# First attention of a decoder layer: loop body rotated by half a tile on all engines, output projection in the values' bank, residual sum and normalisation behind the query remainder

## The chip, the cores and the metric

The kernel runs on one core of a Trainium2 chip. Its time is the device time of one execution in microseconds, from the profiler's clock; the lower the better. Each engine works through its own queue in order: TensorE (PE, matrix products and transposes, results in the PSUM banks), VectorE (DVE), ScalarE (ACT), GpSimd (POOL) and SyncE (SP, which only issues transfers here). They wait for each other by counting semaphores.

## What is computed

A decoder layer on x (16 sequences of 64 tokens, 512 wide, float32): two attentions and a clustered dense layer, each followed by a residual sum and a normalisation. The change lies in the first attention alone.

```python
def attn(x, Wq, Wk, Wv, Wo):            # 32 query heads, 8 key/value heads, 16 wide
    xq = rope((x @ Wq).reshape(b, s, 32, 16))
    xk = rope((x @ Wk).reshape(b, s, 8, 16))
    xv = (x @ Wv).reshape(b, s, 8, 16)
    xk, xv = repeat(xk, 4), repeat(xv, 4)
    scores = where(causal, einsum('bqhd,bkhd->bhqk', xq, xk) / 4, -inf)
    out = einsum('bhqk,bkhd->bqhd', softmax(scores), xv).reshape(b, s, 512)
    return out @ Wo

x = layernorm(x + attn(x, Wq1, Wk1, Wv1, Wo1))
x = layernorm(x + xattn(x, ctx, ...))   # 32 heads of 128, then the dense layer
```

## The kernel before

The tokens are cut into 8 tiles of 128 (two sequences each, T = 8). Every float32 product is made of three passes on operands that are split into a high and a low part: ScalarE writes the high part (a rounding copy, the helper `copy`, L1010), VectorE or GpSimd the low part, the remainder (`low`, L1611, on VectorE). So nearly every operand of TensorE passes through a pair such as `p_high` and `p_low`.

For one tile t of the first attention the steps are these, with the names of the code.
- `a_stage` transposes x, `x_high` and `x_low` split it, `b_stage` multiplies it by Wq (bank 1, L518), `kv_stage` by Wk and Wv (bank 2).
- VectorE's `rope_q` and `rope_k` form the two products of the rotation, GpSimd adds them (query_sum, L1407; key_sum, L1411). ScalarE stacks the high parts, VectorE's `q_low` (128x1024, both inputs in SBUF) and GpSimd's key_low (L1414) the remainders. `v_raw` is copied out by ScalarE (value_raw below), SP moves it to `v_st`, ScalarE (value_high) and GpSimd (value_low, L1428) split it. value_raw of a tile waits for value_low of the tile before it (`s_vl`).
- `qk_stage` turns queries and keys in six groups of four transposes (L575; q0, q1, k0, q2, q3, k1) in banks 0, 3 and 4, and ScalarE copies each group out.
- `s_stage` makes the scores of units 0 and 1 (S01) and of units 2 and 3 (S23), L599. Each unit is 128x512 elements of softmax: a causal copy and a maximum on VectorE (`masked_max`), a subtraction on GpSimd (`sub`), an exponential on ScalarE (`expo`), a sum with reciprocal on VectorE (`total`), a scaling on GpSimd (`norm`, L1394). `pt_stage` transposes the probabilities (L535) into banks 3 and 4, `p_high` and `p_low` split them.
- `pv_stage` multiplies them by the values (bank 7, L549), `at_high` and `at_low` split the result, `wo_stage` is the output projection (bank 0), `add1` the residual sum, `stats1`, `moments1`, GpSimd's `root1` and `norm1` the normalisation, `x1_stage`, `x1_high` and `x1_low` (bank 2) its transposed, split form for the second attention.

The order on every engine is written out by hand, in a `tile_steps(i)` for each. Tiles 0 and 1 are written out, tiles 2 to 6 are a loop on all engines, tile 7 is written out. With v = i - 1 and w = i - 2, body i on TensorE begins with the query product, runs pt(v, 0), pt(v, 1), kv(i), pt(v, 2), pt(v, 3), the transposes of x for tile i + 1 and those of queries and keys of i, then S01(i), the values of v, x1 of w, S23(i), and ends with the output projection of v. So the softmax of a tile is spread over two bodies.

A period is named here by S01(i): it lasts from the start of S01(i) to that of S01(i + 1). S01(1) starts at 44.16 us, S01(7) at 165.84.

## Time and profile before

| | us |
|---|---|
| three runs, median | 802.83 |
| three runs, lowest and highest | 800.33, 805.8 |
| profiled execution, its own time | 803.76 |
| its span | 801.6 |
| TensorE busy | 760.9 (95%) |
| VectorE busy | 596.9 (74%) |
| ScalarE busy | 322.1 (40%) |
| GpSimd busy | 401.3 (50%) |
| S01(1) to S01(7), first attention | 121.7 |

The first attention takes about the first quarter of the span, the second attention most of the rest. Busy shares are means over both, and the change touches only the first; so the shares to look at are those of single periods, which the rows below show. A busy time is the union of an engine's operations, which overlap by some hundredths of a microsecond: two VectorE operations of 0.68 us one behind the other start 0.60 apart.

### The profile page before, as it was taken

Reading aid. Unit: us, or ns where it says so; the run is one execution under the profiler, and the core shown is the slowest. Engines: PE = TensorE matmul, PEld = TensorE weight load, DVE = VectorE, ACT = ScalarE, POOL = GpSimd, SP = SyncE. Lnnn points to the kernel's source line nnn. Section 1 sums busy time; section 2 is a strip of 40 time slices with the busy share of each in tenths; the row PEclk is TensorE's granted clock in tenths of the full one; section 3 lists DMA queues with packets and bytes.
Section 4 is the critical chain, followed back from the end, with each engine's and each line's share of the span. In section 5 each row is a group of like instructions: output and inputs, shape, how many; then the busy total and the mean of one; then the engine's idle time right before and its main releaser. Section 6 shows DMA issues by size and latency. Waiting matters only on the chain.

```text
span 801.6 us, 13879 instructions
## 1 busy us (share of the span) xinstructions
PE 760.9 (95%) x4809; PEld 650.8 (81%) x4809; DVE 596.9 (74%) x1143; ACT 322.1 (40%) x684; POOL 401.3 (50%) x381
## 2 busy tenths in 40 slices
PE   6889999989989999999999999999999999999996
PEld 4777777779878887888888888888888888888875
DVE  4778888877777676777677667766766777688777
ACT  4455555563333333242333324233333323334335
POOL 7656666674644554444446444444644544445303
PEclk9799999999999999999999999999999999999999
DMA  7710003012352222322222232222233222131002
GB/s 182 190 35 18 16 16 121 3 56 54 71 141 80 53 59 60 103 71 52 78 52 52 71 105 60 52 78 52 52 76 106 54 53 79 27 102 31 1 1 105
DMA packets 107875, 53.54 MB, mean 67 GB/s; under 512 B 80449, under 2 KB 96961, under 8 KB 107841
## 3 DMA queue, kind: packets, MB, share of 16 engines
q1 hardware_dynamic: 107008, 51.51, 25.1%
q10 hardware_dynamic: 576, 1.05, 0.4%
q0 software_dynamic: 256, 0.52, 0.3%
q8 instruction: 21, 0.34, 0.2%
q14 instruction: 14, 0.11, 0.0%
HBM read 32.62 MB, written 2.10 MB: 43 GB/s over the span
## 4 chain that ended last, share of the span: by engine, by line
PE 69%; DVE 15%; issue 5%; POOL 4%; ACT 2%; DMA 2%; SPq 1%; DVEq 0%; POOLq 0%; ACTq 0%
PE bank L743 19%; PE bank L678 16%; PE bank L494 10%; DVE arena_r L1611 5%; PE s_bank L757 4%; PE bank L549 3%; PE s_bank L759 2%; PE bank L727 2%; PE bank L575 2%; DVE small L1699 2%; PE bank L901 2%; DVE arena_f L1693 1%; PE s_bank L727 1%; ACT arena_r L1010 1%; PE s_bank L599 1%
## 5 line engine op out<-in xcount | busy, mean ns | idle before, releaser
L743 PE MATMUL bank<-arena_r 128*128 128x512 f32 x768 | 191.5, 398 | 0.0
L1010 ACT ACTIVATE arena_r<-bank 128x256 fp32r<-128x256 f32 (+2 forms) x249 | 105.0, 459 | 214.4 <-PE bank L710 84.7
L678 PE MATMUL bank<-arena_r 128*128 128x512 f32 x720 | 185.2, 400 | 2.9 <-POOL arena_r L1454 2.4
L743 PEld LDWEIGHTS bank<-arena_r 128*128 128x128 f32 x768 | 139.7, 188 | 26.9
L678 PEld LDWEIGHTS bank<-arena_r 128*128 128x128 f32 x720 | 130.6, 188 | 32.2 <-POOL arena_r L1454 2.8
L494 PE MATMUL bank<-arena_r 128*128 128x256 f32 (+1 forms) x1056 | 147.7, 296 | 2.4 <-DVE arena_r L1611 1.6
L494 PEld LDWEIGHTS bank<-arena_r 128*128 128x128 f32 x1056 | 138.1, 192 | 9.7 <-DVE arena_r L1611 2.2
L1611 DVE TENSOR_TENSOR arena_r<-bank,arena_r 128x256 fp32r<-128x256 f32 (+2 forms) x217 | 99.6, 485 | 54.1 <-ACT arena_r L1010 53.8
L1010 ACT ACTIVATE arena_r<-arena_f 128x512 fp32r<-128x512 f32 (+2 forms) x178 | 104.6, 637 | 58.6 <-DMA arena_f<-arena_f 45.5
L1611 DVE TENSOR_TENSOR arena_r<-arena_f,arena_r 128x512 fp32r<-128x512 f32 (+1 forms) x95 | 87.4, 929 | 16.9 <-ACT arena_r L1010 16.9
L1445 POOL TENSOR_TENSOR arena_f<-arena_f 128x512 f32<-128x512 f32 x30 | 39.2, 1306 | 115.5 <-DVE arena_f L1780 115.4
L1478 POOL TENSOR_TENSOR arena_f<-arena_f,small 128x512 f32<-128x512 f32 x32 | 43.2, 1350 | 62.2 <-DVE small L1849 62.2
L1473 POOL TENSOR_TENSOR arena_f<-arena_f,small 128x512 f32<-128x512 f32 x32 | 33.6, 1049 | 69.4 <-DVE small L1843 66.1
L1806 DVE TENSOR_TENSOR arena_f<-bank,arena_f 128x512 f32<-128x512 f32 x64 | 43.7, 683 | 28.3 <-PE bank L743 28.3
L757 PE MATMUL s_bank<-arena_r 128*128 128x128 f32 x256 | 57.4, 296 | 1.4 <-DVE arena_r L1611 1.4
L1010 ACT ACTIVATE arena_f<-s_bank 128x512 f32<-128x512 f32 (+1 forms) x34 | 19.9, 586 | 95.2 <-PE s_bank L759 90.9
L759 PE MATMUL s_bank<-arena_r 128*128 128x64 f32 x256 | 57.9, 245 | 0.0
L1837 DVE TENSOR_TENSOR arena_f<-s_bank,arena_f 128x512 f32<-128x512 f32 x32 | 22.1, 691 | 46.9 <-ACT arena_f L1010 46.9
L1010 ACT ACTIVATE arena_r<-s_bank 128x512 fp32r<-128x512 f32 (+1 forms) x100 | 52.8, 528 | 5.9 <-PE s_bank L876 3.3
L757 PEld LDWEIGHTS s_bank<-arena_r 128*128 128x128 f32 x256 | 49.0, 191 | 3.3 <-issue 2.2
L759 PEld LDWEIGHTS s_bank<-arena_r 128*128 128x128 f32 x256 | 49.1, 192 | 1.1
L1611 DVE TENSOR_TENSOR arena_r<-s_bank,arena_r 128x512 fp32r<-128x512 f32 (+1 forms) x84 | 48.5, 577 | 1.7 <-ACT arena_r L1010 1.4
(164 smaller groups left out, 1187.1 us busy)
## 6 DMA issues: line engine op xcount, KB each, us to landing
arena_f<-arena_f SPq DMA_DIRECT2D x120, 128.0 KB, 2.5
arena_f<-in_L_xattn_Wo SPq DMA_DIRECT2D x8, 1024.0 KB, 5.4
arena_f<-in_L_xattn_Wq SPq DMA_DIRECT2D x14, 512.0 KB, 4.0
arena_f<-in_x SPq DMA_DIRECT2D x8, 256.0 KB, 3.0
arena_f<-in_x SPq DMA_DIRECT2D x1, 2048.0 KB, 10.2
arena_f<-in_L_xattn_Wk SPq DMA_DIRECT2D x8, 256.0 KB, 3.0
arena_f<-in_L_xattn_Wv SPq DMA_DIRECT2D x8, 256.0 KB, 3.3
arena_f<-in_ctx SPq DMA_DIRECT2D x8, 256.0 KB, 3.3
```

The source lines that it names most:

```text
L494: mm = pe.matmul(bank, lhs(a, c), rhs(b, c), start=(c == 0 and n == 0), stop=(c == chunks - 1 and n == 2))
L678: mm = pe.matmul(BQ2[f][:], w2q_s[a][:, e, j, f, :], xT[b][:, e, tok], start=(e == 0 and n == 0), stop=(e == EC - 1 and n == 2))
L727: mm = pe.matmul(bank[s][:, 0:256], v2[c % 2][a][rows, i, :], pT2[b][rows, i, :], start=(n == 0), stop=(n == 2))
L743: mm = pe.matmul(BO2[i][:], at2[a][:, h, i * P:(i + 1) * P], w2o_s[b][:, h, :], start=(h == 0 and n == 0), stop=(h == HG - 1 and n == 2))
L757: pe.matmul(BS2[h][:, at:at + 2 * S], high, kT2[:, :, b * S:(b + 1) * S], start=True, stop=False, skip_group_check=True)
L759: mm = pe.matmul(BS2[h][:, at + S:at + 2 * S], low_, kT2[:, 0, b * S:(b + 1) * S], start=False, stop=True, skip_group_check=True)
L1010: act.activation(dst, src, ACT.Copy).then_inc(done, 1)
L1445: pool.tensor_tensor(u1q[:, 0], u1q[:, 0], u2q[:, 1], ALU.subtract).then_inc(c_qs, 1)
L1473: pool.tensor_tensor(cut(p2, b=8, k=S), cut(sc2, b=8, k=S), bcast(mx2, 2, S), ALU.subtract).then_inc(c_sub, 1)
L1478: pool.tensor_tensor(cut(p2, b=8, k=S), cut(p2, b=8, k=S), bcast(sm2, 2, S), ALU.mult).then_inc(c_pn, 1)
L1611: dve.tensor_tensor(dst, src, f32(high), ALU.subtract).then_inc(done, 1)
L1806: dve.tensor_tensor(y, banks[6 + i][:], y, ALU.add).then_inc(c_acc, 1)
```

## The change

All four engines get a new `tile_steps`. Body i now begins at S01(i). It holds the whole softmax of tile i, the product, rotation, remainders and transposes of tile i + 1 (which end it on TensorE and ScalarE), and the values and output projection of i - 1. What came before the first S01 is written out in `first_steps`. The loop runs over tiles 2 to 5; tile 6 is written out too. Four more things move:
- The output projection of tiles 0 to 5 goes to bank 7, where the values' products were made, in place of bank 0 (`out_bank`). It no longer waits for a copy of turned queries to leave bank 0; in its place the next `pv_stage` waits for `add1` of the tile before (`s_res`), and `qk_stage` loses that wait.
- On VectorE the four causal copies and maxima are no longer in pairs; `rope_q` of the next tile stands behind the maxima of units 0 and 1, `rope_k` before the last sum, `q_low` between `p_low` 1 and 2.
- `add1`, `stats1` and `moments1` of tile i - 1 stand behind `p_low` 3, then `x_low` of tile i + 2 and `norm1`, one body earlier than before.
- On ScalarE `expo` 2 and 3 stand behind `p_high` 0 and 1. On GpSimd `value_low` stands behind `norm` 3.

```diff
--- before.py
+++ after.py
...
@@ -540,8 +552,10 @@
                     if first:
                         pe.wait_ge(r_table, 2)
                     pe.wait_ge(s_vl, v + 1)
-                    if not first:
+                    if is_last(v):
                         pe.wait_ge(s_al, v)
+                    elif not first:
+                        pe.wait_ge(s_res, v)
                 pe.wait_ge(s_pl, 4 * v + 2 * half_ + 2)
                 for j in range(2 * half_, 2 * half_ + 2):
                     for n, (a, k) in enumerate(PASSES):
@@ -559,8 +573,6 @@
                 pe.wait_ge(s_ql, t + 1)
                 if isinstance(t, int) and t == 1:
                     pe.wait_ge(r_table, 1)
-                if tile_stages(t)[2]:
-                    pe.wait_ge(s_res, t - 1)
                 for j, (kind, n) in enumerate((("q", 0), ("q", 1), ("k", 0), ("q", 2), ("q", 3), ("k", 1))):
                     if j == 2:
                         pe.wait_ge(s_kl, t + 1)
@@ -579,11 +591,11 @@
                 pe.wait_ge(s_al, v + 1)
                 if first:
                     pe.wait_ge(s_w1ol, HG)
-                if t is None:
+                if is_last(v):
                     pe.wait_ge(s_res, v)
-                else:
+                elif is_last(t):
                     pe.wait_ge(s_qke, 6 * t + 4)
-                product(TX[:], lambda a, c: at1[a][:, c, :, :].rearrange("p b q -> p (b q)"),
+                product(out_bank(v)[:], lambda a, c: at1[a][:, c, :, :].rearrange("p b q -> p (b q)"),
                         lambda b, c: w1out[b][:, 2 * (c % 2) + c // 2, :], 4).then_inc(s_wo, 1)
...
@@ -620,39 +632,51 @@
...
+            def first_steps():
+                b_stage(0, True)
+                kv_stage(0, True)
+                pe.wait_ge(s_rq, 1)
+                a_stage(1)
+                qk_stage(0, True)
             def tile_steps(i):
+                following, ahead, old, oldest = tile_stages(i)
                 v, w = i - 1, i - 2
+                s_stage(i, (0, 1), not old)
+                if not following:
+                    pv_stage(v, 0, False)
+                    pv_stage(v, 1, False)
+                    x1_stage(w, i)
+                    s_stage(i, (2, 3), False)
+                    wo_stage(v, i, False)
+                    return
+                b_stage(i + 1, False)
+                s_stage(i, (2, 3), not old)
+                if oldest:
+                    x1_stage(w, i)
                 if old:
                     pv_stage(v, 0, not oldest)
                     pv_stage(v, 1, not oldest)
+                else:
+                    table_turn()
+                pt_stage(i, 0)
                 if oldest:
+                    pe.wait_ge(s_x1l, i - 1)
+                else:
+                    pe.wait_ge(s_rk, i + 1)
+                    pe.wait_ge(s_vr, i + 1)
+                kv_stage(i + 1, False)
+                pt_stage(i, 1)
+                if ahead:
+                    pe.wait_ge(s_rq, i + 2)
+                    a_stage(i + 2)
                 if old:
                     wo_stage(v, i, not oldest)
+                pt_stage(i, 2)
+                pt_stage(i, 3)
+                qk_stage(i + 1, False)
...
@@ -810,10 +834,12 @@
             a_stage(0)
             warm(4)
             pe.wait_ge(s_init, 3)
+            first_steps()
             tile_steps(0)
             tile_steps(1)
-            with pe.Fori(2, T - 1) as t:
+            with pe.Fori(2, T - 2) as t:
                 tile_steps(t)
+            tile_steps(T - 2)
             tile_steps(T - 1)
 
 
...
+            def first_steps():
+                first_high(0)
+                key_high(0)
+                value_raw(0)
+                for h in range(HG):
+                    w1out_high(h)
+                turned_copies(0)
+
+            def tile_steps(i):
+                following, ahead, old, oldest = tile_stages(i)
+                v, w = i - 1, i - 2
                 if not following:
                     wq_high(0, 2)
                     wq_high(0, 3)
+                    at_high(v, False)
+                    expo(i, 0)
+                    expo(i, 1)
+                    value_high(i)
+                    x1_keep(w)
+                    x1_high(w)
+                    wkv_high(0, 0)
+                    wkv_high(0, 1)
+                    expo(i, 2)
+                    expo(i, 3)
+                    return
+                expo(i, 0)
+                if oldest:
+                    x1_high(w)
+                expo(i, 1)
+                first_high(i + 1)
                 if old:
                     at_high(v, not oldest)
+                else:
                     table_copy(0)
                     table_copy(1)
+                p_high(i, 0, not old)
+                expo(i, 2)
+                p_high(i, 1, not old)
                 expo(i, 3)
+                if ahead:
+                    x_high(i + 2)
+                key_high(i + 1)
+                value_high(i)
+                if oldest:
+                    x1_keep(w)
+                p_high(i, 2, not old)
+                value_raw(i + 1)
+                p_high(i, 3, not old)
+                if not ahead:
+                    wq_high(0, 0)
+                    wq_high(0, 1)
+                turned_copies(i + 1)
             def x1_high(w, bank=banks[2]):
                 act.wait_ge(s_x1T, w + 1)
...
+            def tile_steps(i):
+                following, ahead, old, oldest = tile_stages(i)
+                v, w = i - 1, i - 2
+                sub(i, 0, not old)
+                sub(i, 1, not old)
+                if not following:
+                    norm(i, 0)
+                    value_low(i)
+                    sub(i, 2, False)
+                    norm(i, 1)
+                    sub(i, 3, False)
+                    return
+                query_sum(i + 1)
+                norm(i, 0)
+                norm(i, 1)
                 sub(i, 2, not old)
                 sub(i, 3, not old)
+                norm(i, 2)
+                key_sum(i + 1)
+                norm(i, 3)
+                value_low(i)
+                key_low(i + 1)
+                if not ahead:
+                    wq_low(0, 0)
+                    wq_low(0, 1)
+                if old:
+                    root1(v)
             def sum_first(u, j):
...
@@ -1661,7 +1743,7 @@
 
             def add1(v):
                 dve.wait_ge(s_wo, v + 1)
-                dve.tensor_tensor(residual(v), banks[0][:], residual(v), ALU.add).then_inc(s_res, 1)
+                dve.tensor_tensor(residual(v), out_bank(v)[:], residual(v), ALU.add).then_inc(s_res, 1)
 
             def stats1(w):
                 dve.wait_ge(s_res, w + 1)
@@ -1677,6 +1759,8 @@
 
             def norm1(w):
                 dve.wait_ge(s_lp, w + 1)
+                if not is_first(w):
+                    dve.wait_ge(s_x1c, w)
                 dve.tensor_scalar(x1n, residual(w), mv[:, 0:1], rstd, ALU.subtract, ALU.mult).then_inc(s_x1n, 1)
 
             def x1_low(w, bank=banks[2]):
...
+            def first_steps():
+                rope_q(0, True)
+                rope_k(0, True)
+                q_low(0)
+                for h in range(HG):
+                    dve.wait_ge(s_w1oh, h + 1)
+                    low(w1out[1][:, h, :], w1out_raw[:, h, :], w1out[0][:, h, :], s_w1ol)
+                x_low(1)
             def tile_steps(i):
+                following, ahead, old, oldest = tile_stages(i)
                 v, w = i - 1, i - 2
+                if not following:
+                    masked_max(i, 0, False)
                     norm1(w)
+                    masked_max(i, 1, False)
                     wq_low(0, 2)
                     at_low(v)
+                    total(i, 0)
+                    masked_max(i, 2, False)
+                    total(i, 1)
+                    x1_low(w)
+                    wq_low(0, 3)
+                    add1(v)
+                    masked_max(i, 3, False)
+                    return
+                masked(i, 0, not old)
+                masked(i, 1, not old)
+                largest(i, 0)
+                largest(i, 1)
+                rope_q(i + 1, False)
+                masked(i, 2, not old)
                 total(i, 0)
                 total(i, 1)
                 if oldest:
                     x1_low(w)
+                largest(i, 2)
+                masked_max(i, 3, not old)
+                if old:
+                    at_low(v)
+                total(i, 2)
+                rope_k(i + 1, False)
+                total(i, 3)
+                p_low(i, 0)
+                p_low(i, 1)
+                q_low(i + 1)
+                p_low(i, 2)
+                p_low(i, 3)
+                if old:
                     add1(v)
+                    stats1(v)
+                    moments1(v)
+                if ahead:
+                    x_low(i + 2)
+                    if old:
+                        norm1(v)
...
```

GpSimd, the loop body. L1389 is `sub`, L1394 `norm`, L1407 query_sum, L1411 key_sum, L1414 key_low, L1428 value_low, L1399 `root1`; before:

```order
L1394 TENSOR_TENSOR arena_f<-arena_f,small 128x512 [waits s_rc]
L1406 REGISTER_ALU
L1407 TENSOR_TENSOR arena_f<-arena_f 128x512 [waits s_rq]
L1393 REGISTER_ALU
L1394 TENSOR_TENSOR arena_f<-arena_f,small 128x512 [waits s_rc]
L1411 TENSOR_TENSOR arena_f<-arena_f 128x128 [waits s_rk]
L1414 TENSOR_TENSOR arena_r<-arena_f,arena_r 128x32x16 [waits s_kh]
```

The same end of the body in the change; the lines are L1453 for `norm`, L1466 key_sum, L1476 value_low, L1471 key_low, L1458 `root1`:

```order
L1453 TENSOR_TENSOR arena_f<-arena_f,small 128x512 [waits s_rc]
L1466 TENSOR_TENSOR arena_f<-arena_f 128x128 [waits s_rk]
L1453 TENSOR_TENSOR arena_f<-arena_f,small 128x512 [waits s_rc]
L1475 REGISTER_ALU
L1476 TENSOR_TENSOR arena_r<-arena_f,arena_r 128x8x32 [waits s_vh]
L1471 TENSOR_TENSOR arena_r<-arena_f,arena_r 128x32x16 [waits s_kh]
L1457 ISA
L1458 TENSOR_TENSOR small<-small 128x1 [waits s_ln]
```

value_low has moved from behind norm 0 to a place between the last norm and key_low.

VectorE, from the last sum of a tile on, in the change's loop body. L1789 and L1791 are `total`, L1693 the remainders (p_low 0, 1; q_low, 128x32x32; p_low 2, 3; x_low, 128x512), L1746 `add1`:

```order
L1789 TENSOR_REDUCE small<-arena_f 128x8 [waits s_ex]
L1791 RECIPROCAL small<-small 128x8 [waits s_sum]
L1693 TENSOR_TENSOR arena_r<-bank,arena_r 128x2x2x128 [waits s_ph]
L1693 TENSOR_TENSOR arena_r<-s_bank,arena_r 128x2x2x128 [waits s_ph]
L1693 TENSOR_TENSOR arena_r<-arena_f,arena_r 128x32x32 [waits s_qh]
L1693 TENSOR_TENSOR arena_r<-bank,arena_r 128x2x2x128 [waits s_ph]
L1693 TENSOR_TENSOR arena_r<-s_bank,arena_r 128x2x2x128 [waits s_ph]
L1746 ISA [waits s_wo]
L1746 TENSOR_TENSOR arena_f<-bank,arena_f 128x512
```

Before, rope_k, `add1` and q_low stood between p_low 1 and p_low 2.

ScalarE, the change's loop body from key_high on (value_high is 128x8x32, the copy of x1 128x512, value_raw 128x128, p_high 128x2x2x128):

```order
L1036 ACTIVATE arena_r<-arena_f 128x32x16 [waits s_ks]
L1113 REGISTER_ALU
L1036 ACTIVATE arena_r<-arena_f 128x8x32 [waits s_pv,d_v]
L1036 ISA [waits s_x1n]
L1036 ACTIVATE arena_f<-arena_f 128x512
L1036 ACTIVATE arena_r<-bank 128x2x2x128 [waits s_pt]
L1036 ACTIVATE arena_f<-bank 128x128 [waits s_vl,s_rk]
L1036 ACTIVATE arena_r<-s_bank 128x2x2x128 [waits s_pt]
```

value_raw, with its wait for value_low (`s_vl`), now stands between p_high 2 and p_high 3; before it stood behind p_high 3.

## Rows read from the trace of the kernel before

**Rows 1.** Busy time by stretch; columns: stretch, its length, PE, PEld, DVE, ACT, POOL busy (operations), PEclk, DMA share, GB/s.

```profile
44.16:64.33 20.17, 18.14 (x138) 15.52 (x137) 16.62 (x32) 10.92 (x21) 12.17 (x12) 1.00 0.09 19
84.67:104.99 20.32, 18.52 (x142) 15.92 (x141) 17.99 (x36) 11.90 (x23) 12.84 (x13) 1.00 0.08 16
145.63:165.84 20.21, 18.08 (x137) 15.48 (x136) 18.11 (x37) 12.60 (x25) 14.96 (x15) 1.00 0.03 3
...
34.10:37.10 3.00, 2.97 (x16) 2.71 (x16) 2.93 (x8) 2.12 (x5) 2.91 (x3) 0.63 0.43 91
```

**Rows 2.** Timeline, TensorE, tile 1's kv and one steady period; columns: start, us, ..., idle before.

```profile
34.51 2.59 PE L494 MATMUL bank<-arena_r 128*128 128x256 f32 x12
...
84.67 0.29 PE L599 MATMUL bank<-arena_r 64*128 64x64 f32 x1
...
96.65 1.68 PE L494 MATMUL bank<-arena_r 128*128 128x256 f32 x12
99.09 0.65 PE L535 MATMUL bank<-ident,arena_f 128*128 128x128 f32 x4 [0.77 <-DVE arena_r L1611]
99.96 0.66 PE L535 MATMUL s_bank<-ident,arena_f 128*128 128x128 f32 x4 [0.22 <-POOL arena_f L1394]
...
101.80 1.26 PE L575 MATMUL bank<-ident,arena_r 128*128 128x128 f32 x8 [0.74 <-DVE arena_r L1611]
...
104.99 0.29 PE L599 MATMUL bank<-arena_r 64*128 64x64 f32 x1
```

**Rows 3.** Timeline, VectorE, the same period: masked, maximum, rope_q, sum, p_low, rope_k, add1, q_low, p_low(3).

```profile
85.98 0.75 DVE L1693 COPY_PREDICATED arena_f<-causal,s_bank 128x512 f32<-128x512 int32 x1 [0.44 <-PE bank L599]
86.77 0.69 DVE L1695 TENSOR_REDUCE small<-arena_f 128x8 f32<-128x512 f32 x1
...
96.19 0.69 DVE L1628 TENSOR_TENSOR arena_f<-bank,rope 128x512 f32<-128x512 f32 x1
...
97.46 0.68 DVE L1699 TENSOR_REDUCE small<-arena_f 128x8 f32<-128x512 f32 x1
...
98.29 0.67 DVE L1611 TENSOR_TENSOR arena_r<-bank,arena_r 128x512 fp32r<-128x512 f32 x1
...
99.47 0.28 DVE L1639 TENSOR_TENSOR arena_f<-bank,rope 128x128 f32<-128x128 f32 x1
...
99.94 0.68 DVE L1664 TENSOR_TENSOR arena_f<-bank,arena_f 128x512 f32 x1
100.53 1.21 DVE L1611 TENSOR_TENSOR arena_r<-arena_f,arena_r 128x1024 fp32r<-128x1024 f32 x1
...
102.27 0.68 DVE L1611 TENSOR_TENSOR arena_r<-s_bank,arena_r 128x512 fp32r<-128x512 f32 x1
```

**Rows 4.** Timeline, GpSimd, the same period: value_low, norm(3), key_low.

```profile
92.08 0.74 POOL L1428 TENSOR_TENSOR arena_r<-arena_f,arena_r 128x256 fp32r<-128x256 f32 x1
...
98.86 1.05 POOL L1394 TENSOR_TENSOR arena_f<-arena_f,small 128x512 f32<-128x512 f32 x1
...
101.30 1.59 POOL L1414 TENSOR_TENSOR arena_r<-arena_f,arena_r 128x512 fp32r<-128x512 f32 x1 [0.74 <-ACT arena_r L1010]
```

**Rows 5.** Timeline, ScalarE, the same period: p_high(3) and value_raw.

```profile
101.13 0.58 ACT L1010 ACTIVATE arena_r<-s_bank 128x512 fp32r<-128x512 f32 x1
101.60 0.27 ACT L1010 ACTIVATE arena_f<-bank 128x128 f32<-128x128 f32 x1
```

**Rows 6.** Tile 1's q_low, key_sum and key_low; last, all key_sums to 190 us (min/median/max ns).

```profile
38.64 1.22 DVE L1611 TENSOR_TENSOR arena_r<-arena_f,arena_r 128x1024 fp32r<-128x1024 f32 x1
...
38.68 1.50 POOL L1411 TENSOR_TENSOR arena_f<-arena_f 128x128 f32<-128x128 f32 x1 [0.16 <-DVE arena_f L1642]
40.92 1.26 POOL L1414 TENSOR_TENSOR arena_r<-arena_f,arena_r 128x512 fp32r<-128x512 f32 x1 [0.74 <-ACT arena_r L1010]
...
L1411 POOL TENSOR_TENSOR arena_f<-arena_f x8: 447/461/1498, 14.6 to 160.9; 128x128 f32<-128x128 f32 x8
```

**Rows 7.** Groups of instructions, 12 to 190 us, the query product (idle time before it at the end).

```profile
L518 PE MATMUL bank<-arena_r 128*128 128x512 f32 x84 | 21.9, 413 | 0.0
```

190 lines of the change are left out of this document (60 added, 130 removed).

## The prediction

> **What bounds the kernel now.** I read the busy time by stretch first. Cut at the starts of the first score products S01(i), the loop of the first attention shows one period per tile [rows 1]. The steady one is 20.32 us long, with TensorE busy 18.52 and VectorE 17.99, at the full granted clock, 2.4 GHz. So two engines have between them hardly any slack: a perfect rotation could take off 20.32 - 18.52 = 1.8 us a tile and no more. The first attention's periods between S01(1) and S01(7) are six; the most that the change could give is about 6 x 1.8 = 11 us of 802. Everything after S01(7) runs the same code in nearly the same order.
>
> Where TensorE's 1.8 us go, its timeline tells [rows 2]: 0.77 us before the third transpose of the probabilities, 0.22 before the fourth, 0.74 before the query transposes, all ended by VectorE or GpSimd. VectorE's timeline of the same period [rows 3] and the two others [rows 4, 5] give the lengths that the new order is laid out with. VectorE: a causal copy followed by its own maximum 0.79 us from start to start (86.77 - 85.98); a 512-wide operation 0.60 (0.68 less an overlap of 0.08); a sum with its reciprocal 0.83 (98.29 - 97.46); the query rotation 1.27 (97.46 - 96.19); the key rotation 0.47 (99.94 - 99.47); the query remainder q_low, 128x1024, 1.21. From p_low(3) to the next S01 it is 104.99 - 102.27 = 2.72 us, a tail of the last four of the six groups of query and key transposes, which the change keeps.
>
> **The parts.** No arithmetic is removed or added: all multiplications, copies and transfers are the same in number. What changes is who stands behind whom.
>
> *The loop edge and the query/key work.* In the new body the rotations, remainders and transposes of tile i+1 stand behind the softmax of tile i, so that TensorE always has the product of the queries, the values and the output projection to do while the softmax runs. Laid out on VectorE from S01(i) at 0: first causal copy at 1.31 (85.98 - 84.67 [rows 2, 3]); four copies, three of them not followed by their own maximum, 3 x 0.67 + 0.79 = 2.80; four maxima 2.40; query rotation 1.27; four sums 3.4; x1_low and at_low 1.20; key rotation 0.47; p_low(0) and (1) 1.20. That is 14.05. I add 0.2 for two short waits (the rotation behind the query product, which TensorE finishes about then, and the fourth sum behind its exponential): q_low starts at 14.2 and, at 1.21, ends at 15.4.
>
> *What stands beside q_low.* This is the place that decides. GpSimd's queue now has norm(2), key_sum, norm(3), value_low, key_low. norm(3) waits for the fourth sum (13.1), takes 1.05 [rows 4] and ends at about 14.3, so value_low is due just as q_low runs. In the trace of before, a GpSimd operation due during q_low stands until q_low ends: key_sum, 0.46 us at the median, took 1.50 when it was issued at 38.68 beside the q_low of 38.64 to 39.86, and ended 0.32 after it; key_low took 1.59 at 101.30, beside the q_low that ends at 101.74, against 1.26 with VectorE's port free [rows 3, 4, 6]. It ended 1.15 after q_low, 0.11 less than its own time. So value_low (0.74) ends at 15.4 + 0.63 = 16.05. ScalarE's value_raw(i+1) waits for it, and p_high(3) stands behind value_raw: 16.05 + 0.05 + 0.17 (0.27 less an overlap of 0.1) = 16.3; p_high(3) takes 0.58 [rows 5] and ends at 16.85; p_low(3) on VectorE starts at 16.9; with the tail of 2.72 the next S01 comes at 19.6. The period is 19.6 against 20.32: 0.7 us gained. If q_low were the one to be held (norm(3) or value_low first), it would start at 14.3 or at 15.1 and p_low(3) at 16.9 or 16.7; the period stays at 19.5 to 19.6.
>
> The Trainium skill speaks against the change here ("SBUF — State Buffer", section on the two separate sides): VectorE and GpSimd share a port pair, held exclusively for a whole instruction, which a VectorE operation with two SBUF inputs and a GpSimd operation contend for. By that, the trace agrees: 1.50 against 0.46. A plan that overlooks the rule would come out at the 19.0 us period of the first rival.
>
> *Other engines in the period.* TensorE: S01, query product, S23, x1 transposes, values, and so on to the output projection sum to 15.1 us (18.5 less the 3.2 of the query transposes and a little for gaps), before q_low is done; the idle time that is left lies in front of and between the query transposes. Cost of moving: none, cover: VectorE's chain. The output projection moves to bank 7 and loses its wait for a turned copy; it now waits for at_low, at about 10.9, and TensorE comes to it at 11.4. If at_low came 0.5 later, pt(2) and pt(3) would be late next. The residual sum, statistics and x_low stand behind p_low(3): 16.9 + 0.6 + 0.8 + 0.4 + 0.6, the root in GpSimd, norm1 0.46, together to about 20.4. The next first causal copy is due at 19.6 + 1.3 = 20.9. That is free, with 0.5 us of room. SP's transfers of the values start at value_raw, 16.3, one period ahead of the value_high that needs them at 14: free.
>
> *Tile 0.* Here the new order costs. Before, sums and probabilities of tile 0 ran while TensorE did the query product for tile 1 at a low clock. Now the rotation of tile 1 stands ahead of them in VectorE's queue, and exp(3) on ScalarE stands behind p_high(1), which stands behind kv(1) on TensorE; that kv took 2.59 us before [rows 2], in a stretch whose granted clock is 0.63 on the mean, between the levels of 1.2 and 2.4 GHz [rows 1]. TensorE idles some 2 us in that place again. I get exp(3) at 37.5, p_low(0) at 39.0, q_low from 40.2 to 41.4, value_low 42.05, p_low(3) 42.9, S01(1) at 45.6 where it is 44.16 now [rows 1]: 1.4 us lost. With kv(1) at the full clock (1.68 [rows 2]) it is 0.6.
>
> *Tile 1* has no x1 work; 20.17 becomes about 19.5: 0.7 gained. *Tiles 2 to 5*: 4 x 0.7 = 2.9. *Tile 6*: ScalarE puts two wq copies of 0.55 each (128x512 like p_high) between p_high(3) and the copies of the turned queries, which TensorE's fourth transpose group waits for: 19.6 + 0.5 = 20.1 against 20.21: 0.1. *The edge of the loop*: five iterations become four, one body unrolled. On TensorE the branch now lies between query transposes and S01; I cost it at nothing, since the groups of lines show no idle time at all before the query product, which stands at the edge now [rows 7]. It can't give time; how much it can cost is the third rival.
>
> **Sum**: -1.4 + 0.7 + 2.9 + 0.1 = 2.3 us gained. Against the profiled execution's 803.8 that is 801.5; the median of the three runs shown is 802.8, 1.0 below it, and so 800.5. The runs of before reach from 800.3 to 805.8, so that a difference below 1% (8 us) is about what a measurement of this kernel can't tell from no change.
>
> **The rivals.**
> 1. *The port is not held where I think* (norm(3) early, q_low late, or value_low done while p_low(1) runs). Then value_low ends at 15.1, p_high(3) follows p_high(2) at 15.6, p_low(3) starts at 16.25 and the period is 19.0, 1.3 gained per tile. Tile 0 loses 0.6, tile 1 gains 1.3, four tiles 5.4, tile 6 0.8: 6.9 us, a median of 796. For it: 0.1 to 0.5 us of error in my 14.2 is possible. Against it: norm(3) is tied to the fourth sum, and q_low follows that sum by only 2.0 us on VectorE, so both shift together. Chance 0.22, with a third of it above 1% by the spread of the runs.
> 2. *Nothing changes*: exp(2) and exp(3) stand behind p_high(0) and (1) on ScalarE now, which stand behind transposes on TensorE, which stand behind norm(0), x1_low and kv. My margins are small: the fourth sum has 0.02 us. Each link that is 0.3 late adds 0.3 to each period; with 0.5 per tile over six tiles the gain of 2.3 is gone: 803. Chance 0.15.
> 3. *Slower, by the edge of the loop.* TensorE's loop body is some 140 products and as many weight loads, and its branch lay behind the twelve products of the output projection, some 2.8 us of queued work that hid whatever a branch costs. Now only four transposes, 0.44 us, lie between it and S01, and S01's scores start everything. So the bound is between 0 and 2.83 - 0.44 = 2.4 us on each of three branches back: up to 7.2 us. At more than 0.8 us each the gain is gone; at the full bound the median is 807.7. Against it: ScalarE's branch, behind exp(3), shows no gap either. The Trainium skill names a mechanism ("Runtime: NRT & Kernel Launch", on instruction fetch): a taken branch to a page that isn't held forces a fetch before execution goes on. No row here shows such a stall. Chance 0.13, and 0.04 of it, with other mishaps in tile 0, over 1% slower.
>
> **Chances and range.** My forecast 0.50, the rivals 0.22, 0.15 and 0.13. The range takes in rival 1 with a run 1.5 us below its 796, and from above rival 2 and half of rival 3: 794.5 to 805. Over 1% faster (below 794.8) 0.13: a third of rival 1 and 0.06 for lengths that I took too long. Over 1% slower 0.06. Within 1%: 0.81.
>
> **What would show it.** Right: a steady period near 19.6 us; value_low drawn out to 1.3 us or more beside q_low, p_high(3) ended by GpSimd, tile 0's period longer than 21.4, tile 6's about 20.1; no gap in front of S01 in tiles 3 to 6 that tile 2 doesn't have. A period of 19.0 with value_low at 0.74 is rival 1. A gap in front of S01 at three tile boundaries alone is rival 3. A period above 20 with idle time in front of kv or pt(1) is rival 2, and would make the forecast wrong.

## The result, and the profile after

The changed kernel took **799.11 us** (median of 20 runs, 795.83 to 807.45) beside 803.08 us for the kernel before (20 runs): a ratio of 0.9959, 95% interval 0.9942 to 0.9975. That is 4 us (2 to 5 by the interval). The forecast was 800.5 in a range of 794.5 to 805.0, and no change above 1%. The profiled span is 799.6 us against 801.6. Every ratio below is against runs of the kernel before in the same series, whose medians were 802.50 to 804.43.

The starts of the first score products S01(i), read from TensorE's timeline of each kernel, give the periods; the last column is what comes behind S01(7).

| | S01(0) at | tile 0 | tile 1 | tiles 2 to 5 | tile 6 | behind S01(7) |
|---|---|---|---|---|---|---|
| before | 22.77 | 21.39 | 20.17 | 20.32 to 20.33 | 20.21 | 635.8 |
| after | 23.20 | 23.07 | 19.47 | 19.92 to 19.96 | 19.90 | 634.2 |
| forecast | - | 22.8 | 19.5 | 19.6 | 20.1 | 635.8 |

Behind S01(1) the six periods take 119.10 us instead of 121.68, 2.58 less. Tile 0 takes 1.68 of it back. So the part that was forecast, S01(0) to S01(7), gained 0.9 and not 2.3. The 0.9 holds for these two profiles, which both ran tile 1's query product at the low clock. A second profile of the kernel before, shown below, has it at the full clock and a tile 0 of 19.26 us; against that one the changed kernel is slower in this part. Only the periods behind S01(1) are alike in both.

The busy time of three stretches of after, in the columns of [rows 1]: a steady period, tile 1's and tile 6's.

```profile
85.69:105.62 19.93, 18.52 (x143) 15.78 (x142) 17.88 (x36) 11.89 (x23) 13.35 (x14) 1.00 0.09 16
46.27:65.74 19.47, 18.04 (x138) 15.38 (x138) 16.05 (x33) 11.08 (x21) 12.73 (x13) 1.00 0.07 18
145.47:165.37 19.90, 18.34 (x137) 15.31 (x136) 17.64 (x35) 12.41 (x24) 15.83 (x16) 1.00 0.05 6
```

TensorE is busy for the same 18.52 us, VectorE for 17.88 against 17.99. VectorE's timeline of the steady period answers to [rows 3]: the rotation of the queries, the fourth sum, p_low(0) and (1), q_low, p_low(2) and (3), then the residual sum.

```profile
89.85 0.69 DVE L1710 TENSOR_TENSOR arena_f<-bank,rope 128x512 f32<-128x512 f32 x1 [0.32 <-PE bank L530]
...
98.15 0.69 DVE L1789 TENSOR_REDUCE small<-arena_f 128x8 f32<-128x512 f32 x1
...
98.99 0.64 DVE L1693 TENSOR_TENSOR arena_r<-bank,arena_r 128x512 fp32r<-128x512 f32 x1
99.55 0.68 DVE L1693 TENSOR_TENSOR arena_r<-s_bank,arena_r 128x512 fp32r<-128x512 f32 x1
100.14 1.25 DVE L1693 TENSOR_TENSOR arena_r<-arena_f,arena_r 128x1024 fp32r<-128x1024 f32 x1
101.32 0.69 DVE L1693 TENSOR_TENSOR arena_r<-bank,arena_r 128x512 fp32r<-128x512 f32 x1
102.88 0.69 DVE L1693 TENSOR_TENSOR arena_r<-s_bank,arena_r 128x512 fp32r<-128x512 f32 x1 [0.86 <-ACT arena_r L1036]
103.48 0.68 DVE L1746 TENSOR_TENSOR arena_f<-bank,arena_f 128x512 f32 x1
```

GpSimd's timeline beside it (norm(3), value_low, key_low; against [rows 4]):

```profile
99.27 1.04 POOL L1453 TENSOR_TENSOR arena_f<-arena_f,small 128x512 f32<-128x512 f32 x1
100.36 1.62 POOL L1476 TENSOR_TENSOR arena_r<-arena_f,arena_r 128x256 fp32r<-128x256 f32 x1
101.95 1.26 POOL L1471 TENSOR_TENSOR arena_r<-arena_f,arena_r 128x512 fp32r<-128x512 f32 x1
```

ScalarE's (value_raw, p_high(3); against [rows 5]):

```profile
102.08 0.28 ACT L1036 ACTIVATE arena_f<-bank 128x128 f32<-128x128 f32 x1 [0.79 <-POOL arena_r L1476]
102.25 0.59 ACT L1036 ACTIVATE arena_r<-s_bank 128x512 fp32r<-128x512 f32 x1
```

And TensorE's, the turned probabilities (3), then the query and key groups up to S01 (against [rows 2]):

```profile
100.37 0.66 PE L547 MATMUL s_bank<-ident,arena_f 128*128 128x128 f32 x4
101.45 1.27 PE L587 MATMUL bank<-ident,arena_r 128*128 128x128 f32 x8 [0.42 <-DVE arena_r L1693]
103.71 0.63 PE L587 MATMUL s_bank<-ident,arena_r 128*128 128x128 f32 x4 [0.99 <-DVE arena_r L1693]
104.18 1.04 PE L587 MATMUL bank<-ident,arena_r 128*128 128x128 f32 x8
105.05 0.63 PE L587 MATMUL s_bank<-ident,arena_r 128*128 128x128 f32 x4
```

Read across, this is one chain. value_low, 0.74 us in [rows 4], is drawn out to 1.62 beside q_low and ends at 101.98; value_raw starts at 102.08 after a wait that the trace puts down to it; p_high(3) follows at 102.25, p_low(3) at 102.88 after a wait of 0.86 for ScalarE, and the next S01 2.74 later, at 105.62. TensorE, which stood before three of its groups in [rows 2], now stands before two, for 0.42 and 0.99 us. The row of GpSimd's line for value_low over the whole program (duration of one, least, median and most, in ns, and who waited) shows that it is so in seven of the eight tiles. The one of 737 ns is that of tile 7, behind which no query remainder stands:

```profile
L1476 POOL TENSOR_TENSOR arena_r<-arena_f,arena_r x8: 737/1622/1790, 40.2 to 173.1; 128x256 fp32r<-128x256 f32 x8
...
  ACT arena_f L1036: 6.0, 7
```

### The profile page after: what moved, and what is told of

Its sections match the earlier page's. It is cut to its first block, busy times and chain, and to the rows that moved or that the text cites. A ratio compares the mean times of both kernels' runs of the same rounds, so it can differ in the third digit from the quotient of the medians.

```text
span 799.6 us, 13805 instructions
## 1 busy us (share of the span) xinstructions
PE 762.1 (95%) x4809; PEld 650.7 (81%) x4809; DVE 597.0 (75%) x1143; ACT 322.8 (40%) x684; POOL 403.7 (50%) x381
## 4 chain that ended last, share of the span: by engine, by line
PE 65%; DVE 14%; POOL 9%; issue 6%; ACT 3%; DMA 2%; SPq 1%; DVEq 0%; POOLq 0%; ACTq 0%
PE bank L767 18%; PE bank L702 15%; PE bank L506 10%; PE s_bank L781 4%; DVE arena_r L1693 3%; PE s_bank L783 2%; PE bank L530 2%; POOL arena_f L1453 2%; PE bank L751 2%; PE bank L927 2%; DVE small L1789 2%; POOL arena_r L1476 2%; ACT arena_r L1036 1%; PE s_bank L751 1%; DVE arena_f L1777 1%
## 5 line engine op out<-in xcount | busy, mean ns | idle before, releaser
L1693 DVE TENSOR_TENSOR arena_r<-bank,arena_r 128x256 fp32r<-128x256 f32 (+2 forms) x217 | 99.5, 485 | 43.3 <-ACT arena_r L1036 42.4
L1036 ACT ACTIVATE arena_r<-arena_f 128x512 fp32r<-128x512 f32 (+1 forms) x178 | 103.9, 638 | 59.9 <-DMA arena_f<-arena_f 44.6
L1693 DVE TENSOR_TENSOR arena_r<-arena_f,arena_r 128x512 fp32r<-128x512 f32 (+1 forms) x95 | 88.9, 944 | 15.9 <-ACT arena_r L1036 15.6
L1558 POOL TENSOR_TENSOR arena_f<-arena_f,small 128x512 f32<-128x512 f32 x32 | 43.7, 1367 | 60.8 <-DVE small L1951 60.8
L1553 POOL TENSOR_TENSOR arena_f<-arena_f,small 128x512 f32<-128x512 f32 x32 | 33.6, 1050 | 69.2 <-DVE small L1945 65.9
L1693 DVE TENSOR_TENSOR arena_r<-s_bank,arena_r 128x512 fp32r<-128x512 f32 (+1 forms) x84 | 48.6, 579 | 6.8 <-ACT arena_r L1036 6.6
L781 PEld LDWEIGHTS s_bank<-arena_r 128*128 128x128 f32 x256 | 49.0, 191 | 3.3 <-POOL arena_r L1630 1.4
L1448 POOL TENSOR_TENSOR arena_f<-arena_f,small 128x512 f32<-128x512 f32 x32 | 33.6, 1063 | 32.7 <-DVE small L1781 32.7
```

Source lines behind the costliest of these rows:

```text
L781: pe.matmul(BS2[h][:, at:at + 2 * S], high, kT2[:, :, b * S:(b + 1) * S], start=True, stop=False, skip_group_check=True)
L1036: act.activation(dst, src, ACT.Copy).then_inc(done, 1)
L1448: pool.tensor_tensor(cut(p1[u], b=8, k=S), cut(sc1[u % 2], b=8, k=S), bcast(mx1[u], 2, S), ALU.subtract).then_inc(s_sub, 1)
L1553: pool.tensor_tensor(cut(p2, b=8, k=S), cut(sc2, b=8, k=S), bcast(mx2, 2, S), ALU.subtract).then_inc(c_sub, 1)
L1558: pool.tensor_tensor(cut(p2, b=8, k=S), cut(p2, b=8, k=S), bcast(sm2, 2, S), ALU.mult).then_inc(c_pn, 1)
L1693: dve.tensor_tensor(dst, src, f32(high), ALU.subtract).then_inc(done, 1)
```

## The experiments

Theory: GpSimd's value remainder, held up beside q_low, stands between q_low and p_high(3) and so sets the period. The main rival: the period is set elsewhere, by q_low itself or by TensorE's loop edge, and the long value_low only lies beside it.

**The value copy last.** ScalarE's value_raw, the only one that waits for value_low, behind p_high(3):

```diff
-                value_raw(i + 1)
                 p_high(i, 3, not old)
+                value_raw(i + 1)
```

> The changed kernel, but with value_raw of the next tile behind p_high(3) on ScalarE in place of ahead of it. Theory (value_low held beside q_low sets the period, through value_raw): p_low(3) follows p_low(2) at once, 0.86 us earlier, but the key group of the transposes then waits for key_low, which ends at 103.21 in the changed kernel's trace where the group starts at 103.71; so the steady period falls from 19.93 to about 19.5, and the time by 5 x 0.45 = 2 us against the change. Rival (VectorE's own chain sets the period, the wait is slack): period stays at 19.9.

Measured: 795.09 us, ratio 0.9907 (0.9873 to 0.9941); steady periods 19.51 to 19.55 as the theory had it, tile 1 19.07, tile 6 19.44. value_low is as long as in the changed kernel, but p_high(3) no longer stands behind the one that waits for it. GpSimd's row of value_low, and TensorE's timeline, which shows what is late next: key_low, which stands behind value_low on GpSimd.

```profile
94.76 1.63 POOL L1476 TENSOR_TENSOR arena_r<-arena_f,arena_r 128x256 fp32r<-128x256 f32 x1
...
95.85 1.27 PE L587 MATMUL bank<-ident,arena_r 128*128 128x128 f32 x8 [0.43 <-DVE arena_r L1693]
97.67 0.65 PE L587 MATMUL s_bank<-ident,arena_r 128*128 128x128 f32 x4 [0.55 <-POOL arena_r L1471]
```

Two lines exchanged on one engine gave 0.4 us a tile; the wait on value_low is the one that sets the changed kernel's period.

**The value remainder early.** value_high behind p_high(0) on ScalarE and value_low ahead of norm(2) on GpSimd, out of q_low's way:

```diff
                 p_high(i, 0, not old)
+                value_high(i)
                 expo(i, 2)
...
                 key_high(i + 1)
-                value_high(i)
...
+                value_low(i)
                 norm(i, 2)
                 key_sum(i + 1)
                 norm(i, 3)
-                value_low(i)
                 key_low(i + 1)
```

> The changed kernel, but with value_high behind p_high(0) on ScalarE and value_low behind the last subtraction on GpSimd, away from q_low. Theory (the collision of value_low with q_low): value_low takes 0.74 us in place of 1.62, key_low is now the one held beside q_low and ends at about 102.8 on the clock of the changed kernel's trace, the key group starts at about 102.9 in place of 103.71, steady period 19.1, against the change -4 us. Rival (any GpSimd operation beside q_low costs the same, only its name changes): key_low ends at 103.6 and the period stays at 19.9. Rival (norm(2) and norm(3), 0.35 us later, hold the transposes): period 19.6.

Measured: 793.62 us, ratio 0.9872 (0.9841 to 0.9904); steady periods 19.21 to 19.25, tile 1 18.49, tile 6 19.08. GpSimd's timeline, with value_low, norm(3) and key_low:

```profile
91.75 0.75 POOL L1476 TENSOR_TENSOR arena_r<-arena_f,arena_r 128x256 fp32r<-128x256 f32 x1
...
93.88 1.05 POOL L1453 TENSOR_TENSOR arena_f<-arena_f,small 128x512 f32<-128x512 f32 x1
94.88 2.27 POOL L1471 TENSOR_TENSOR arena_r<-arena_f,arena_r 128x512 fp32r<-128x512 f32 x1
```

VectorE's, with q_low and p_low(2), (3):

```profile
94.49 1.52 DVE L1693 TENSOR_TENSOR arena_r<-arena_f,arena_r 128x1024 fp32r<-128x1024 f32 x1
95.93 0.68 DVE L1693 TENSOR_TENSOR arena_r<-bank,arena_r 128x512 fp32r<-128x512 f32 x1
96.53 0.67 DVE L1693 TENSOR_TENSOR arena_r<-s_bank,arena_r 128x512 fp32r<-128x512 f32 x1
```

value_low has its own length back, key_low is held in its place (2.27 against 1.26) where the transposes don't need it yet, and p_low(3) waits for nobody. The theory had a period of 19.1. q_low itself has grown to 1.52, beside norm(3), which ends 0.44 after q_low starts; with q_low at its 1.21 of [rows 3] the period would, by my estimate, be 0.3 shorter, near the 19.0 of the first rival. No run shows that.

**The residual sum ahead of q_low, projection in bank 0.** The two other parts of the change undone, in the new loop body, and with the bank its waits, which the diff doesn't show; statistics and normalisation stay where the change has them:

```diff
-            return banks[0] if isinstance(v, int) and v >= T - 2 else banks[7]
+            return banks[0]
...
                 p_low(i, 1)
+                if old:
+                    add1(v)
                 q_low(i + 1)
                 p_low(i, 2)
                 p_low(i, 3)
                 if old:
-                    add1(v)
                     stats1(v)
```

> The changed kernel, but with the output projection of all tiles in bank 0 as before, its waits as before, and the residual sum add1 ahead of q_low on VectorE (statistics and normalisation stay behind p_low(3)). Theory: the bank and the place of the residual sum buy nothing while value_low sets the period: q_low comes 0.6 us later, value_low then runs ahead of it unhindered (0.74) or holds it for 0.3, and p_low(3) starts within 0.2 us of where it does in the change; period 19.9 +- 0.2, the same time as the change within 1 us. Rival (each operation ahead of q_low lengthens the period): 20.5, 3 us slower than the change.

Measured: 796.49 us, ratio 0.9924 (0.9896 to 0.9952); steady periods 19.71 to 19.82, 0.1 to 0.2 shorter than in the changed kernel, not longer, tile 1 19.30 and tile 6 19.38 (19.90 there). The rival is refuted; the theory has the period, but not the time, which it put within 1 us of the change. VectorE's and GpSimd's timelines say why:

```profile
95.98 0.69 DVE L1746 TENSOR_TENSOR arena_f<-bank,arena_f 128x512 f32 x1
96.59 1.32 DVE L1693 TENSOR_TENSOR arena_r<-arena_f,arena_r 128x1024 fp32r<-128x1024 f32 x1
```

```profile
96.10 0.73 POOL L1476 TENSOR_TENSOR arena_r<-arena_f,arena_r 128x256 fp32r<-128x256 f32 x1
96.79 2.26 POOL L1471 TENSOR_TENSOR arena_r<-arena_f,arena_r 128x512 fp32r<-128x512 f32 x1
```

The 0.6 us of the sum put q_low so late that value_low slips in ahead of it, unhindered. TensorE's query transposes start 0.06 us behind q_low, and no group behind them waits, so here q_low sets the period. So bank 7 and the residual sum behind the query remainder together gain nothing in this loop body: the earlier q_low meets value_low, and that costs a little more than it saves. Which share the bank has wasn't measured apart. With value_low out of the way, as in the second experiment, the order of the change is 0.5 us a tile shorter than this one (19.2 against 19.7).

**The changed kernel once more**, for the stretch behind S01(7), in the same series as the three experiments above:

> The changed kernel once more, for a second profile. Theory A (the 1.5 us that the stretch behind S01(7) took less than in the profile of before are chance, from transfers that land late in some executions): this stretch is between 634 and 636 us, the periods S01(1) to S01(7) the same as in the first profile within 0.1 us each. Theory B (the second attention gains from the change): it is 634.2 again.

Measured: 799.91 us, ratio 0.995 (0.9926 to 0.9975), periods 23.05, 19.48 and 19.92 to 19.96 again, behind S01(7) 634.2 again. That fits both theories, since A's range of 634 to 636 holds 634.2; the next profile of the kernel before decides between them.

Against these 799.91 us the three kernels above took 4.8, 6.3 and 3.4 us less, where their periods from S01(1) to S01(7) are 2.5, 4.7 and 1.5 shorter in the profiles. The rest of 1.6 to 2.3 us lies outside these six periods. All three had tile 1's query product at the full clock in their profile, the changed kernel had not in either of its two; whether the orders bring that about or chance does, no run here shows. The periods, not the medians, are what the readings above rest on.

**Tile 0, the first two sums ahead.** In tile 0 alone:

```diff
-                query_sum(i + 1)
+                if old:
+                    query_sum(i + 1)
                 norm(i, 0)
                 norm(i, 1)
+                if not old:
+                    query_sum(i + 1)
...
+                    masked_max(i, 0, True)
+                    masked_max(i, 1, True)
+                    total(i, 0)
+                    total(i, 1)
+                    rope_q(i + 1, False)
+                    masked(i, 2, True)
```

> Tile 0 alone is re-ordered on VectorE and GpSimd: the first two sums stand ahead of the rotation of tile 1's queries, and query_sum behind norm(0) and norm(1). Theory A (tile 0 is lost by the order: sums behind the rotation and the last exponential behind the key copy): S01(1) comes 0.5 to 3.5 us earlier behind S01(0) than the 23.05 us of the changed kernel, its TensorE idles less than 1.0 us ahead of the key and value product where it idled 2.07, and the steady periods stay at 19.9; ratio to the kernel before 0.990 to 0.995. Theory B (tile 0's length is set by where TensorE's low clock falls in the start-up, whatever the order): the period of tile 0 is 22.5 to 23.1 if the query product of tile 1 runs at the low clock as it did before, and about 20 if it runs at the full one; the idle time does not matter; ratio 0.995 again or, with the full clock, 0.992.

Measured: 800.18 us, ratio 0.997 (0.995 to 0.9991); tile 0 21.27 us, with the query product at the full clock (3.02 us), steady periods 19.91 to 19.95. Theory A had the period and the steady ones and TensorE's idle time before the product of keys and values, which is gone, but not the ratio; and its 23.05 was measured at the low clock, so that the period doesn't confirm it. Theory B asked for about 20 at the full clock and got 1.3 more. The idle time has moved: TensorE now stands 5.34 us before the third group of transposes. ScalarE's timeline shows the new wait: the high part of the queries waits 3.60 us for query_sum, and exp(2) stands behind it in the queue.

```profile
30.61 1.06 ACT L1036 ACTIVATE arena_r<-arena_f 128x1024 fp32r<-128x1024 f32 x1 [3.60 <-POOL arena_f L1462]
...
33.00 0.64 ACT L1075 ACTIVATE arena_f<-arena_f 128x512 f32<-128x512 f32 x1
```

query_sum itself waits for VectorE, not for the norms ahead of it: the second norm ends at 29.08, query_sum starts at 29.28, behind the end of the rotation at 29.21. The rotation is late because it now stands behind two sums, each of which waits some 0.45 us for its exponential.

**The early value remainder and this order together:**

> The early value remainder of the kernel that measured 0.987, and tile 0's sums first. Theory A (the order in tile 0 costs by itself): 0.5 to 2 us less than that kernel's 20.18 in the period of tile 0, steady periods 19.2, ratio 0.984 to 0.987. Theory B (tile 0 is set by the clock): period of tile 0 as there, 20.2, or 22 to 23 if the low clock falls into the query product of tile 1; ratio 0.987 to 0.990.

Measured: 794.38 us, ratio 0.9894 (0.9863 to 0.9925); steady 19.21 to 19.25, tile 0 21.16. Theory A asked for less than 20.18 and got 1.0 more; theory B had 20.2 or 22 and more, and neither came. This order of the sums is no cure for tile 0.

**The kernel before, a second profile:**

> The kernel before once more, one look. The stretch behind S01(7), 635.8 us before and 634.2 in both profiles of the changed kernel. Theory A (the 1.6 us are the change's, by the state in which it leaves transfers and buffers): 635.5 to 636. Theory B (chance, by when staging transfers land): anything from 633.5 to 636.5, with other waits than 2.41 and 1.74 us. Periods 20.3 for tiles 2 to 5 and 20.2 for tiles 1 and 6 by both; tile 0 21.4 with the query product of tile 1 at the low clock, 2 us less without.

Measured: 801.03 us (span 799.0), periods 19.26, 20.15, 20.31 to 20.34, 20.22; behind S01(7) 636.2. The 636.2 is 0.2 above theory A's range and in B's; TensorE's two waits that B expected to differ, 2.41 and 1.74, are 2.58 and 1.77. That speaks for A. And it is the same program, with tile 0 at 19.26 where it had 21.39. The granted clock of the same four microseconds in the first profile of before and in this one (the column before the last two, in the order of [rows 1]):

```profile
24.00:28.00 4.00, 4.00 (x16) 3.26 (x15) 2.77 (x4) 0.55 (x1) 1.29 (x2) 0.50 1.04 383
```

```profile
24.00:28.00 4.00, 3.47 (x30) 2.76 (x29) 3.48 (x6) 1.53 (x3) 2.69 (x3) 1.00 1.04 388
```

At 0.50, the level of 1.2 GHz, tile 1's query product took 4.61 us; at 1.00, 2.4 GHz, 3.02.

**The fourth exponential of tile 0 ahead of p_high(1)**, in the changed kernel and in the one with the early value remainder:

```diff
                 expo(i, 2)
+                if not old:
+                    expo(i, 3)
                 p_high(i, 1, not old)
-                expo(i, 3)
+                if old:
+                    expo(i, 3)
```

> The changed kernel, with the fourth exponential of tile 0 put ahead of p_high(1) on ScalarE. Theory A (in tile 0 the last exponential behind p_high(1), which stands behind the key and value product, delays the fourth sum and with it everything to S01(1)): VectorE's wait of 0.65 us before the fourth sum (1.03 where the key and value product ran longer) is gone, and the period of tile 0 is 0.7 to 1.0 us shorter than in the changed kernel with the same clock: 22.4 with the query product of tile 1 at the low clock (23.07 there), about 19.7 at the full one; steady periods 19.9; ratio to the kernel before 0.994 to 0.995. Theory B (p_low(3), held up through GpSimd's value remainder, or the clock alone decides in tile 0 too): the period is 23.1 or 20.7, nothing gained.

> The early value remainder (ratio 0.987, tile 0 20.18 us, steady periods 19.2) with the fourth exponential of tile 0 ahead of p_high(1). Theory A: period of tile 0 19.1 to 19.4 with the query product of tile 1 at the full clock, 0.8 to 1.0 less than without the swap; ratio 0.986. Theory B: 20.2 again, ratio 0.987. By both the steady periods are 19.2.

Measured: 798.87 us, ratio 0.995 (0.9923 to 0.9977), tile 0 19.47; and 790.97 us, ratio 0.9861 (0.9821 to 0.9901), tile 0 18.49, steady 19.20 to 19.24, the lowest ratio of all. The first period is near theory A's 19.7; the second is 0.6 below its 19.1 to 19.4. Neither confirms it, for both profiles had the key and value product at the full clock, and there the swap changes nothing, as the next table shows (all times from the trace of each kernel; the third column of times is from the end of tile 1's query product to the start of the fourth sum of tile 0).

| kernel | query product | key and value product | to the fourth sum | tile 0 |
|---|---|---|---|---|
| before | 4.61 | 2.59 | - | 21.39 |
| before, second profile | 3.02 | 2.21 | - | 19.26 |
| changed | 4.43 | 2.15 | 8.68 | 23.07 |
| changed, residual sum ahead | full clock | 2.79 | 9.25 | 20.72 |
| value remainder early | 3.00 | 2.79 | 9.26 | 20.18 |
| value copy last | full clock | 1.68 | 7.96 | 19.05 |
| changed, exponential swapped | 3.04 | 1.68 | 7.94 | 19.47 |
| value remainder early, swapped | 3.02 | 1.67 | 7.95 | 18.49 |
| sums first | 3.02 | 1.67 | 9.76 | 21.27 |
| value remainder early, sums first | full clock | 1.68 | 10.07 | 21.16 |

With the order of VectorE that the change has, this column follows the key and value product whatever the order of the exponentials: 7.95 with it at 1.68, with and without the swap. So exp(3), behind p_high(1), behind that product, costs 0.7 to 1.3 us where the product runs at the low clock, and nothing at the full one. Whether the swap saves those 0.7 us at the low clock stays open: no profile of it fell there. The 18.49 is helped by the clock, which was 1.00 from the query product of tile 1 to the end of tile 0 in this profile alone. That this kernel's ratio is below the one without the swap (0.9861 against 0.9872) is within the intervals. The two kernels with the sums first had both products at the full clock and are still 1.8 and 2.7 us longer in tile 0 than their counterparts without that order (21.27 against 19.47, 21.16 against 18.49): that order costs.

## Why the prediction was right, point by point

**The bound, and value_low beside q_low: right.** It was the place that decides, as said. By the forecast's own clock, from S01 at 0: q_low at 14.45 (14.2 forecast), value_low's end 16.29 (16.05), p_high(3) 16.56 (16.3), p_low(3) 17.19 (16.9), the next S01 19.93 (19.6). Of the 0.33 us that are missing, 0.25 are there at q_low; behind it the steps were right to 0.1 us, the tail 2.74 for 2.72. The mis-sized term is the 12.9 us that I gave VectorE's chain from the first copy (1.31) to q_low: it measured 13.13. The rotation alone waits 0.32 for the query product, where I had 0.2 for all waits together; the rest is in the lengths. q_low is a little longer than 1.21, too (1.25): norm(3) ends 0.17 after q_low begins.

The price is small, but it comes once a tile: four steady periods gained 0.37 to 0.41 each, 1.6 together, where 2.9 was forecast. Tile 1 gained the 0.70 that was forecast. Tile 6 gained 0.31 and not 0.1. The two wq copies on ScalarE do cost there, 3.10 us from p_low(3) to S01(7) and not 2.74, so 0.36 where I had 0.5; but q_low starts 14.08 behind S01(6), 0.37 earlier than in the steady period, which my sum had nothing for.

**The shared port: right.** Taking the collision away gave 0.7 us a tile. VectorE is held as well, which no row of before showed: q_low ends 1.08 us after the GpSimd operation that was there first, in each of three kernels (the changed one, the residual sum ahead, the value remainder early) (norm(3) ends at 100.31, q_low at 101.39; value_low at 96.83, q_low at 97.91; norm(3) at 94.93, q_low at 96.01). By the rule of the Trainium skill ("SBUF — State Buffer", the two separate sides) the port pair is held for a whole instruction; the traces agree, on either engine.

**The first rival** is refuted as to the changed kernel (a period of 19.0, value_low at 0.74) and nearly confirmed as a price: with value_low out of the way the steady period is 19.2, 1.1 below before where the rival had 1.3, and tile 1's 18.49. (Its sum puts four tiles at 5.4, and four times 1.3 is 5.2.) My chance of 0.22 on it rested on an error of up to 0.5 us in the start of q_low; q_low came later than forecast, and norm(3), tied to the same sum, came later with it, as I had argued.

**The second rival**, nothing changes, did not come about: no group of TensorE ahead of the query transposes waits in the steady period. But its worth was half right, by another way: the loop and tile 0 together gave 0.9 us of the 2.3.

**The third rival**, the loop edge, shows nothing. In the changed kernel the last group of transposes starts 0.57 us before S01 at 105.62, with the branch between them; with no branch between them, in the written-out tile 0 of the kernel with the swapped exponential, it is 42.14 and 42.70, 0.56. The fetch on a taken branch that the Trainium skill names ("Runtime: NRT & Kernel Launch", instruction fetch) leaves nothing to be seen here.

**Tile 0**: forecast 1.4 lost, measured 1.68, at the low clock, with S01(1) at 46.27 for 45.6. The idle time before the keys and values was forecast as some 2 us and is 2.07; exp(3) at 37.5, q_low at 40.2 and p_low(3) at 42.9 came at 37.51, 40.15 and 42.84, and the fourth sum waits for exp(3) as I laid out. Some luck is in these, for S01(0) was 0.43 later than before and the chain behind it that much shorter than I had it. The whole 0.67 stands behind p_low(3): the tail took 3.43 us and not 2.72. What I hadn't foreseen is a further stretch at the low clock, where TensorE's query transposes ran; the window of 42 to 44 us:

```profile
42.00:44.00 2.00, 1.46 (x8) 1.06 (x7) 1.16 (x2) 1.75 (x4) 1.18 (x1) 0.50 0.08 8
```

With the full clock I said 0.6 lost; 19.47 (swapped, where the swap changes nothing) against 19.26 is 0.2, and 20.72 against 19.26 is 1.5, each with its own pattern of the clock. A difference of two single profiles in tile 0 says little.

**What the sum left out.** Everything behind S01(7) was taken as unchanged. It is 1.6 us shorter, 634.2 in both profiles of the changed kernel against 635.8 and 636.2. TensorE's waits show where. Before:

```profile
231.24 3.01 PE L678 MATMUL bank<-arena_r 128*128 128x512 f32 x12 [2.41 <-POOL arena_r L1454]
...
309.55 0.44 PE L710 MATMUL bank<-ident,arena_f 128*128 128x128 f32 x2 [1.74 <-POOL arena_f L1478]
```

After:

```profile
230.02 3.04 PE L702 MATMUL bank<-arena_r 128*128 128x512 f32 x12 [1.66 <-POOL arena_r L1534]
...
656.71 0.44 PE L734 MATMUL bank<-ident,arena_f 128*128 128x128 f32 x2 [0.56 <-POOL arena_f L1558]
```

The first wait is shorter, the second is gone and a new one of 0.56 has come. TensorE's idle time, by stretches that are counted from S01(7), is 0.75 us less (40 to 80 us), 1.58 less (120 to 160) and 0.73 more (480 to 560): 1.6 in all. The second wait stands at the end of a chain that ScalarE's timelines, before and then after, show the start of: a transfer of the second attention lands later before.

```profile
305.37 1.15 ACT L1010 ACTIVATE arena_r<-arena_f 128x512 fp32r<-128x512 f32 x2 [5.35 <-DMA arena_f<-arena_f]
```

```profile
301.99 1.16 ACT L1036 ACTIVATE arena_r<-arena_f 128x512 fp32r<-128x512 f32 x2 [3.15 <-DMA arena_f<-arena_f]
```

Counted from S01(7) that is 139.53 and 136.62. The wait is 5.38 in the second profile of before, and 3.1 to 3.2 in all nine profiles with the new body. SP issues the same transfers in the same order in all of them, and why this one lands 2.2 us later stays open.

The stretch behind S01(7) is 633.9 to 635.7 in these nine, and most of this spread is the clock, not the order. In the first experiment and in the one with only tile 0's sums moved it is 635.3 and 635.7, and there the granted clock drops to 0.6 for some four microseconds 70 us before the end: between two TensorE groups that are 13.03 us apart before and 13.09 in the changed kernel, they take 14.66 and 14.68. Up to the first of these groups, counted from S01(7), they are as early as the changed kernel. So the 1.6 us are the new body's, by a way that no one laid out, and a low clock can hide them.

Of the 4.0 us between the medians the two profiles place 2.6 in the loop, minus 1.7 in tile 0, minus 0.4 in the start-up and 1.6 here: 2.1, where the spans differ by 2.0. The other 2 aren't placed by any trace; single executions of one kernel lie further apart than that.

So the number was right in part by luck. The profiled execution was forecast at 801.5 and took 801.41: 1.4 us too much gain in the part that was laid out, and 1.2 too little in the parts that were taken as fixed; the remaining 0.3 lies between span and device time. The median lies 2.3 below that execution, and not 1.0 as before.

## What to carry to other kernels

When an order is re-laid, write both engines of the shared pair side by side with starts and ends: an operation of 0.74 us that becomes due beside one of 1.2 doesn't cost 0.74 but ends 0.6 behind the other, and what counts is who stands behind it. The cheapest cure here wasn't to avoid the overlap but to let nothing urgent stand behind the one that is held: exchanging two lines on ScalarE, so that no copy on the way to the end waits for it, or having another operation held, by one line moved on GpSimd and one on ScalarE, took the change's 0.4% to 0.9% and 1.3%.

Look first at whether a tile's length hangs on the clock before explaining it by the order; the same program gave 21.39 and 19.26 us for one tile.

## What the runs showed of the hardware

- A GpSimd operation that is due while q_low runs ends a fixed time behind it, its own length less 0.12 to 0.15 us: key_low 1.14 behind (own 1.26) in the second and in the third experiment, value_low 0.59 behind (own 0.74) in the changed kernel.
- VectorE is held just as well by a GpSimd operation that was there first: q_low took 1.25, 1.32 and 1.52 us with 0.17, 0.24 and 0.44 us of overlap.
- VectorE's sum of a PSUM bank and an SBUF operand held no one: value_low, started beside `add1` in the third experiment (96.10 and 95.98), took 0.73.
- In the start-up the granted clock differs between executions of one program (0.50 and 1.00 from 24 to 28 us in two profiles of the kernel before), and tile 0 took 21.39 and 19.26 us in them. Near the end a drop to 0.6 cost 1.6 us in two of eleven profiles.
